# The masked product of a pruning pass, made and stored in two halves

## The reference

```python
cos = xn @ xn.T
edge_scores = jax.nn.softmax(cos * H / TAU, axis=1)          # H is adj
edge_mask = (edge_scores >= th_edge) & comp_mask[:, None]
H_pruned = H * edge_mask
connectivity = H_pruned.sum(axis=1)                          # row sums
edeg = jnp.maximum(H_pruned.sum(axis=0), EPS)                # column sums
...                                                          # node mask, dv_isqrt from connectivity
agg = H_pruned.T * dv_isqrt[None, :] @ transformed
agg = agg * (1.0 / edeg)[:, None]
msg = dv_isqrt[:, None] * (H_pruned @ agg)
x = jax.nn.relu(msg @ Theta)
```

## Time and profile before

| what | value |
|---|---|
| time, median of 3 runs | 2391.56 us (2390.45 to 2393.32) |
| the profiled execution's own time | 2393.9 us |
| its span in the profile | 2392.1 us |
| TensorE busy | 2070.8 us, 87% |
| VectorE busy | 1735.0 us, 73% |
| ScalarE busy | 753.9 us, 32% |
| mean granted TensorE clock | 0.936 |
| moved by DMA | 828.91 MB, mean 347 GB/s |

### The profile page before, as it was taken

One profiled execution on the slowest core, in us unless ns is written; L12 is line 12 of the kernel. 1 busy time (PEld: TensorE's weight loads), 2 busy tenths in 40 slices (PEclk: granted clock), 3 DMA queues, 4 the chain that ended last, 5 costly groups with the idle time before them and its releaser, 6 DMA issues. The chain is left out here.

```text
span 2392.1 us, 36030 instructions
## 1 busy us (share of the span) xinstructions
PE 2070.8 (87%) x15658; PEld 736.6 (31%) x15658; DVE 1735.0 (73%) x2056; ACT 753.9 (32%) x869; POOL 4.5 (0%) x18
## 2 busy tenths in 40 slices
PE   7899998899976777799999989987777789997997
PEld 2224333222221111244444323221111134434333
DVE  5996743188889999955541358869999975555998
ACT  0001000066633333211110036643333311112897
POOL 0000000000000000000000000000000000000000
PEclk9999999999988888799999999988888899998999
DMA  9988999899559999977779989919999987775894
GB/s 374 421 352 364 421 428 428 362 404 372 225 240 401 414 387 417 390 267 269 276 301 396 427 365 381 378 74 394 386 412 393 412 323 281 283 283 229 337 420 176
DMA packets 130220, 828.91 MB, mean 347 GB/s; under 512 B 8464, under 2 KB 10512, under 8 KB 76560
## 3 DMA queue, kind: packets, MB, share of 16 engines
q1 hardware_dynamic: 128016, 825.29, 85.9%
q10 hardware_dynamic: 2048, 1.35, 0.2%
HBM read 690.29 MB, written 136.31 MB: 346 GB/s over the span
## 5 line engine op out<-in xcount | busy, mean ns | idle before, releaser
L1183 ACT ACTIVATE stream<-stream,negmax 128x4096 f32<-128x4096 f32 x128 | 475.2, 3713 | 514.0 <-DVE negmax L1177 514.0
L1136 PE MATMUL ps<-edgeT,node_twice 64*128 64x512 f32 x1024 | 284.5, 676 | 172.8 <-DVE mx L1172 172.7
L1172 DVE CUSTOM_DVE_ANT_0 stream<-ps,stream 128x1024 f32<-128x1024 f32 x296 | 347.8, 1220 | 41.5 <-PE ps L1136 27.2
L1136 PE MATMUL ps<-edgeT,query_twice 64*128 64x512 f32 x1024 | 249.5, 619 | 6.0 <-DVE edgeT L1379 3.7
L577 PE MATMUL ps<-stream,moved_block 128*64 128x512 f32 x960 | 216.3, 600 | 25.5 <-DMA stream<-in_adj 25.5
L1650 PE MATMUL ps<-stream,xw 32*64 32x512 f32 x4096 | 229.6, 589 | 2.6 <-issue 2.0
L1136 PEld LDWEIGHTS ps<-edgeT,node_twice 64*128 64x128 f32 x1024 | 95.2, 203 | 366.6 <-DVE mx L1172 260.6
L1154 PE MATMUL ps<-stream,ones 128*1 128x512 f32 x1024 | 187.0, 869 | 9.4 <-DVE stream L1691 9.4
L1217 ACT ACTIVATE query_twice<-ps,less_one_exponent 128x512 int32<-128x512 int32 x256 | 154.9, 687 | 14.4 <-PE ps L1307 12.1
L1691 DVE SCALAR_TENSOR_TENSOR stream<-stream,cut 128x4096 f32<-128x4096 f32 x34 | 152.5, 4485 | 1.2
L1754 DVE STREAM_TRANSPOSE stream<-spare 128x4096 f32<-128x4096 f32 x22 | 97.5, 4432 | 73.8 <-PE ps L1650 52.9
(11 more groups left out here) (233 smaller groups left out, 1954.2 us busy)
## 6 DMA issues: line engine op xcount, KB each, us to landing
stream<-in_adj SPq DMA_DIRECT2D x122, 2048.0 KB, 15.3
stream<-in_adjT SPq DMA_DIRECT2D x69, 2048.0 KB, 15.1
pruned<-stream SPq DMA_DIRECT2D x64, 2048.0 KB, 10.5
spare<-pruned SPq DMA_DIRECT2D x22, 2048.0 KB, 11.5
query_twice<-pruned SPq DMA_DIRECT2D x22, 2048.0 KB, 11.3
spare<-in_adj SPq DMA_DIRECT2D x20, 2048.0 KB, 10.0
moved_block<-in_adj SPq DMA_DIRECT2D x20, 2048.0 KB, 11.0
node_twice<-pruned SPq DMA_DIRECT2D x20, 2048.0 KB, 11.5
```

What stands on the lines that cost most here:

```text
L1136: last = nc.tensor.matmul(ps[:, 2 * slot + h, :], stationary[F * h:F * h + F, rows_n], bank_of(edgeT[F * h:F * h + F, :], c), start=True, ...
L1172: nc.vector.tensor_tensor_reduce(out=prod[s][:, cols], in0=ps[:, 2 * slot:2 * slot + 2, :].rearrange("p a b -> p (a b)"), in1=block_in[:, ...
L1183: nc.scalar.activation(prod[s], prod[s], ACT.Exp, bias=negmax[:, s:s + 1], accum_out=zsum[:, s:s + 1]).then_inc(exp_done, 1)
```

## The change

The masked product of a block is made by two instructions of 128x2048 in place of one of 128x4096. The first writes its row sums to the block's column of `conn`, the second to the block's column of `mean`, a tile of the same shape that is free in the pass. Each raises `pruned` by one, so the counts on it double. SyncE issues a store of 1 MB behind each half, both on the same `stored[s]`, whose counts double too. TensorE's column sums wait for both halves. Before the node step one instruction adds `mean` to `conn`.

```diff
--- before.py
+++ after.py
@@ -1533,15 +1533,17 @@
 
                     def wait_stored(blocks):
                         for s in range(SL3):
-                            sp.wait_ge(stored[s], 16 * len(range(s, blocks, SL3)))
+                            sp.wait_ge(stored[s], 32 * len(range(s, blocks, SL3)))
 
                     def load(n):
                         sp.dma_start(places[n % HELD], adj_b[seq[n]]).then_inc(loaded[n % HELD], 16)
 
                     load(R)
                     for n in range(NB):
-                        sp.wait_ge(pruned, n + 1)
-                        sp.dma_start(Hp[seq[n]], prod[n % SL3]).then_inc(stored[n % SL3], 16)
+                        for half in range(2):
+                            cols = slice(HALF * half, HALF * half + HALF)
+                            sp.wait_ge(pruned, 2 * n + half + 1)
+                            sp.dma_start(Hp[seq[n]][:, cols], prod[n % SL3][:, cols]).then_inc(stored[n % SL3], 16)
                         for m in range(R + 1, NB):
                             if n == m - HELD + (m >= 14) + (m >= 22):
                                 load(m)
@@ -1588,7 +1590,7 @@
                 def _(pe):
                     def column_sum(t):
 
-                        pe.wait_ge(pruned, t.n + 1)
+                        pe.wait_ge(pruned, 2 * t.n + 2)
                         add_column_sums(ones[:, :], prod[t.k % SL3]).then_inc(summed, 1)
 
                     def body(t):
@@ -1688,16 +1690,18 @@
                             in1=st["refuse"][:, bass.ds(t.block, 1)], op0=ALU.mult, op1=ALU.add)\
                             .then_inc(cut_ready, 1)
                         dve.wait_ge(cut_ready, t.n + 1)
-                        nc.vector.scalar_tensor_tensor(
-                            out=prod[s], in0=prod[s], scalar=cut[:, s:s + 1], in1=buffer(t),
-                            op0=ALU.is_ge, op1=ALU.mult,
-                            accum_out=st["conn"][:, bass.ds(t.block, 1)]).then_inc(pruned, 1)
+                        for half, sums in enumerate((st["conn"], st["mean"])):
+                            cols = slice(HALF * half, HALF * half + HALF)
+                            nc.vector.scalar_tensor_tensor(
+                                out=prod[s][:, cols], in0=prod[s][:, cols], scalar=cut[:, s:s + 1],
+                                in1=buffer(t)[:, cols], op0=ALU.is_ge, op1=ALU.mult,
+                                accum_out=sums[:, bass.ds(t.block, 1)]).then_inc(pruned, 1)
 
                     def body(t):
                         s = t.k % SL3
                         if t.k >= R:
                             dve.wait_ge(loaded[t.k % HELD], 16 * (t.turn(HELD, R) + 1))
-                        wait(dve, stored[s], t.turn(SL3) * 16)
+                        wait(dve, stored[s], t.turn(SL3) * 32)
                         wait(dve, summed, t.n - 2)
                         weighted_scores(dve, t, buffer(t), seen, scores_ready, chunk_used, max_ready)
                         if t.k >= 1:
@@ -1705,7 +1709,7 @@
                     for n in range(NB):
                         body(last_step(n, seq))
                     prune(last_step(NB - 1, seq))
-                    dve.wait_ge(pruned, NB)
+                    dve.wait_ge(pruned, 2 * NB)
 
                 @block.scalar
                 def _(act):
@@ -1754,6 +1758,7 @@
                         v.transpose(turned_pair[y % 3][:, N * (x % 2):N * (x % 2) + N], chunk_slot[x % 3])\
                             .then_inc(turned, 1)
 
+                    do(v.tensor_tensor(st["conn"][:, :], st["conn"][:, :], st["mean"][:, :], ALU.add))
                     v.tensor_scalar(st["dv"][:, :], st["conn"][:, :], DEG_EPS, None, ALU.max).then_inc(deg_floor, 1)
                     do(v.tensor_tensor(st["score"][:, :], st["conn"][:, :], st["feat"][:, :], ALU.mult))
                     v.reduce_max(gl["gmax"][:, :], st["score"][:, :], AX.X).then_inc(node_sems["part_max"], 1)
```

## The result

The changed kernel takes 2379.77 us (median of 5 runs, 2377.19 to 2382.16), against 2391.76 us for the kernel before (5 runs, 2390.45 to 2397.44). The ratio is 0.9943, 95% interval 0.9932 to 0.9955: faster by 0.57%, some 13.6 us, where the forecast was 4.2 us. The median lies just inside the range, but the gain is three times the one worked out, so the account behind it was wrong in a term or more.

The account below looks back on a forecast made before the run. The prediction held that in most steps the DMA transfers bound the pass; 0 - 4.4 - 2.0 + 1.9 + 0 = -4.5 us, rounded to -4.2, gave 2387.4 us; main case 2383 to 2392, 8 in 10 from -12 to +4.5 us.

Parts of the forecast that it names:

- (1) VectorE: In both pruning passes, two half products cost VectorE 0.14 us more a block, 9 us, hidden in store waits: counted 0.
- (2) The head start: First store of each pass starts 2.2 us earlier and this lasts to the end: -4.4 us; nothing while queue is full.
- (3) The gaps: Behind n = 8 and 17, where no load is issued, earlier half stores fill 0.5 us each, four gaps: -2.0 us.
- (4) The shape: Store rows of 8 KB in place of 16 KB cost 0.03 us a store, +1.9 us over 64 blocks.
- rival B: Slower: smaller transfers cost the full queue more than their bytes; 0.2 us a block gives +12.8, 2400 us; chance 0.17.
- (5) Nothing from TensorE and the node step: Later column sums and the added sum before the node step are covered: 0, or +0.4 us if uncovered.
- A: Rival: stores' latency holds the pruning loop, so all 29.2 us of VectorE's waits go: -20 us, 2371; chance 0.13.

Follow-up runs that it names:

- six split blocks: Product and store in halves only for n = 0, 1, 9, 10, 18, 19 of each pass, against the kernel before: ratio 0.9972, -6.7 us.
- complementary sets: Against the kernel before, both split: n = 0, 9, 18 only 0.9990, all others 0.9998; n = 0, 1, 9, 10, 18, 19 only 0.9972, all others 0.9987.

## Why the prediction was wrong

- **(1) VectorE: right.** 0.14 us a block was taken, 4.56 - 4.42 = 0.14 us measured, and most of it disappears in the waits, as said: +2.4 us when only that is done, with 0 counted.
- **(2) The head start: the step that failed.** "While the queue is full this gives nothing: the same bytes pass in the same order, and the second half ends where the whole would have." With the queue at share 1.00 and no gap, halves from n = 6 on gave some 10 us. The prediction took the 421 GB/s of one stretch of 70 us at a share of 1.01 as the rate of the full queue in the whole pass, and so left nothing to win. In that stretch, among the first blocks, halves are indeed no faster (419 GB/s), but already there their steps are shorter, 77.6 us for eight in place of 79.2. Later in the pass whole stores move only 409 to 411 GB/s at a share of 1.00, and halves 422 to 426, where no load is left out. VectorE's waits for stores, which the prediction thought bound to the queue's rate and cut only to 16 to 20 us, fell to 4.7 + 4.9 = 9.6. That the first store of a pass, 2.2 us earlier, helps to the end may be right; no run has it alone, and with n = 9 and 18 it gave 2.4 us (0 to 5.0), not 4.4.
- **(3) The gaps: right place, too small.** 0.5 us for each was taken, for the sake of the last engine. In the changed kernel the gap behind n = 8 has (1 - 0.27) x 3 = 2.2 us of idle time left of 3.4, 1.2 us less, and six split blocks gave 6.7 us in all; what a gap alone is worth no run shows. The 10.60 us between the issues of n = 8 and 9, from which the small price was argued, are VectorE's step and say nothing of when the queue's last part landed. The second dry place, one block later, was missed.
- **(4) The shape: too small.** +1.9 us with bounds 0 and 3.8 was taken, +5.5 us (+3.1 to +7.9) measured with the stores alone in halves. This is rival B's mechanism at 0.09 us a block, under its 0.14. The Trainium skill's figures for 1 MB and 16 MB transfers (DMA: Bandwidth & Descriptors, Bandwidth) gave 75 us as an estimate in the prediction; the 5.5 us measured show that it is not so for transfers that follow each other in one queue.
- **(5) Nothing from TensorE and the node step: nothing in the runs speaks against it.**
- **The rivals.** A, at 0.13, was nearest, in mechanism and in size. It said that each earlier store shortens VectorE's wait whatever the queue, and gave -20 us, with part wins from -8. The waits fell by 19.6 us and the longer products cost 9, which leaves 10.6 of the 13.6 us. As worded (waits near 0, 9.5 us throughout) it goes too far: 12 of 30 steps are still longer, up to 10.8 us. And the halves without n = 0, 9 and 18 gave 0.5 us, where it wanted 10 to 12.

So it is shown that halves gain in a full queue, that they need both the split product and the split store, and that VectorE then waits less. How the queue comes to move more is argued, not shown. One account: a transfer is spread over 16 engines, VectorE waits for the last of them before it goes on, and so the next store comes late for those that are ahead; half a store that is there 2.2 us earlier would keep them at work. The other: each store simply lands earlier, VectorE, with three tiles to write into, goes on earlier, and the GB/s only follow its shorter steps. The rows show neither single engines nor what a packet waits for, and the plain test of VectorE's waits, a fourth tile to write into with whole stores, was not run. That stays open, as does why the gains of complementary sets (-2.4 and -0.5, -6.7 and -3.1) don't add up to 13.6.

## What to carry to other kernels

Read a DMA queue's fullness from its GB/s beside its share: two stretches at a share of 1.00 differed by 4% here, and the slower one had something to gain from work that is handed over sooner. Look also at who waits for the landing: a store that lands earlier can be worth something in a full queue, if its maker waits for it. Where a product takes about as long to make as to store (4.5 and 5.0 us here) and its maker waits for stores, try to store it in two halves, each as early as it is done; here splitting only the product or only the store lost. Split every block, not only those before which the queue runs dry, because a whole block behind a split one opens the gap again.

## What the runs showed of the hardware

- 2.1 MB stores in two transfers of 1 MB, with rows of 8 KB and not 16, cost 5.5 us over 64 blocks, 0.09 us a block, when both are issued together.
- At a DMA share of 1.00 over 160 us, without left-out loads, a core moved 409 and 411 GB/s with whole stores and 426 and 422 with halves handed over 2.2 us earlier. The changed kernel, with left-out loads, moved 412 over its whole passes, at the same share.
- Among the first blocks of a pass, at a share of 1.01, whole stores moved 421 GB/s and halves 419.
- Taking the left-out loads back in, which closes both gaps, made the kernel with whole products slower by 4.1 us (1.4 to 6.7) and not faster: at the end of the pass, where only stores are left, the DMA stood idle for 8.4 us of 20.
